# Second mixers of a state-space block: the first group's convolution as matmuls, side work re-laid, the matrix of means as one column

## What is computed

```
xi, z = split(x @ Win)                  # 512 channels each
xi = silu(causal_dwconv(xi, convw) + convb)          # 4 taps a channel
dt, B, C = split(xi @ Wx); dt = softplus(dt @ Wdt + bdt)
h[t] = exp(dt[t] * A) * h[t-1] + dt[t] * xi[t] * B[t]     # 16 states a channel
y[t] = sum over states of C[t] * h[t] + D * xi[t]
out = (y * silu(z)) @ Wout
```

## Time and profile before

| | |
|---|---|
| median of 3 runs | 3392.23 us (3391.65 to 3394.02) |
| profiled execution | 3390.75 us, its span 3389.0 us |
| DVE busy | 2789.4 us, 82% |
| PE busy | 2772.9 us, 82% |
| POOL busy | 2236.3 us, 66% |
| ACT busy | 1774.9 us, 52% |
| TensorE's granted clock, mean | 0.93 |

### The profile page before, as it was taken

The page is one execution under the profiler, slowest core; times in us unless marked ns, Lnnn a source line. Parts: engine busy times, 40 slices in busy tenths (PEclk is TensorE's granted clock), DMA queues, the critical chain, the costliest instruction groups (busy, mean ns, idle before and its releaser), DMA issues. The chain is left out here.

```text
span 3389.0 us, 25111 instructions
## 1 busy us (share of the span) xinstructions
PE 2772.9 (82%) x7782; PEld 1186.5 (35%) x7782; DVE 2789.4 (82%) x2257; ACT 1774.9 (52%) x2375; POOL 2236.3 (66%) x1102
## 2 busy tenths in 40 slices
PE   7678777765778888988888898898898887688999
PEld 2223222454223333333333333333333332244444
DVE  6999999543369999999999999999999999588200
ACT  6775767222355555655655565565556554234211
POOL 3796499001249898898898899898898999301000
PEclk8999799877889999999999999899999999899999
DMA  2011011156625554554554555554545556321000
GB/s 66 31 50 37 21 54 51 37 193 226 217 90 180 172 182 169 182 186 165 190 193 156 196 184 168 174 186 161 201 174 180 193 175 203 112 68 50 13 19 25
DMA packets 164165, 451.46 MB, mean 133 GB/s; under 512 B 22816, under 2 KB 51680, under 8 KB 164000
## 3 DMA queue, kind: packets, MB, share of 16 engines
q1 hardware_dynamic: 158272, 428.89, 37.2%
q0 software_dynamic: 5760, 20.97, 1.5%
HBM read 414.94 MB, written 34.87 MB: 133 GB/s over the span
## 5 line engine op out<-in xcount | busy, mean ns | idle before, releaser
L1424 POOL TENSOR_TENSOR mix_prod<-mix_spread,mix_h 128x1024 f32<-128x1024 f32 x512 | 1352.9, 2645 | 197.3 <-DVE mix_h L1847 101.6
L1957 PE MATMUL mix_banks<-mix_prod,kept_ident 128*128 128x512 f32 x2048 | 1021.8, 624 | 62.9 <-POOL mix_prod L1424 35.7
L1474 ACT ACTIVATE mix_side_in<-mix_dt,kept_neg_a 128x1024 f32<-128x1024 f32 x384 | 437.5, 1141 | 291.0 <-DVE mix_h L1847 287.1
L1957 PEld LDWEIGHTS mix_banks<-mix_prod,kept_ident 128*128 128x128 f32 x2048 | 396.8, 198 | 482.6 <-issue 303.9
L1833 DVE TENSOR_TENSOR mix_banks<-mix_banks,mix_dtu 128x1024 f32<-128x1024 f32 x384 | 466.9, 1216 | 6.0 <-POOL mix_dtu L1414 3.4
L1847 DVE TENSOR_TENSOR_SCAN mix_h<-mix_side_in,mix_state,mix_banks 128x1024 f32<-128x1024 f32 x192 | 450.6, 2347 | 17.8 <-issue 0.4
L1847 DVE TENSOR_TENSOR_SCAN mix_h<-mix_side_in,mix_banks 128x1024 f32<-128x1024 f32 x192 | 439.0, 2286 | 17.3
L451 POOL TENSOR_TENSOR mix_drive<-mix_drive,mix_du 128x1024 f32<-128x1024 f32 x128 | 304.7, 2396 | 149.9 <-ACT mix_drive L521 149.9
L1434 POOL TENSOR_TENSOR mix_side_in<-mix_spread,mix_dtu 128x512 f32<-128x512 f32 x256 | 326.5, 1275 | 0.1
L1947 PE MATMUL mix_banks<-mix_parts,kept_sel 96*128 96x512 bf16 x384 | 154.0, 401 | 209.0 <-DVE mix_h L1847 201.9
L671 DVE TENSOR_TENSOR_SCAN mix_h<-mix_banks,mix_state,mix_drive 128x1024 f32<-128x1024 f32 x128 | 296.1, 2339 | 11.2 <-POOL mix_drive L451 5.8
(11 more groups left out here) (270 smaller groups left out, 4416.4 us busy)
## 6 DMA issues: line engine op xcount, KB each, us to landing
mix_spread<-par_rows SPq DMA_DIRECT2D x640, 512.0 KB, 4.0
mix_c_row<-c_rows SPq DMA_DIRECT2D x40, 512.0 KB, 3.6
exa_f<-f SPq DMA_DIRECT2D x32, 512.0 KB, 6.8
slot_outputs<-kept_early POOLq DMA_DIRECT2D x32, 512.0 KB, 7.3
ln_zp<-slot_outputs SPq DMA_DIRECT2D x8, 2048.0 KB, 8.4
first_acc<-xT SPq DMA_DIRECT2D x8, 512.0 KB, 7.4
x_scratch<-first_acc POOLq DMA_DIRECT2D x8, 512.0 KB, 3.2
fw_scratch<-mix_res SPq DMA_DIRECT2D x8, 512.0 KB, 5.4
```

The costliest lines, as they stand in the source:

```text
L1424: pool.tensor_tensor(prod[:, un % 2, :], spread[:, i % SLOTS, :], h[:, un % HR, :], ALU.mult).then_inc(prod_ready, 1)
L1474: act.activation(drive[un % 2] if pooled(un) else side_in[:, un % 2, :], dt[:, at // NS, :], ACT.Exp, scale=neg_a[:, way(p), at:at + 1]).t ...
L1957: mm = pe.matmul(y_bank[:, hf, :], k.ident[:], half(prod[:, un % 2, :], hf), start=False, stop=True, skip_group_check=True)
```

## The change

- Group 0's convolution is done like group 3's: four diagonal matrices on PE in slots 29 and 30 of the pass before, two evictions by ACT at slots 30 and 31. tap_diag holds two sets of matrices. The taps of group 0 on ACT and DVE are gone; DVE keeps those of groups 1 and 2 (slots 36, 37, 38 and 39, 41, 42).
- The two z products of group 1 go from slots 29, 30 to 31, 32, and silu_z from 31 to 33. gate_y of group 1 stays at 34.
- The input products go from slots 26, 28, 32, 33, 34, 36, 37, 39 to 24, 27, 33, 34, 35, 36, 38, 39, their evictions with them; the second var from 27 to 28, its roots from 28 to 29.
- On DVE root_of of the second half goes from slot 40 to 35, its two normed from 43, 44 to 40, 43, and one joined from 38 to 44.
- The matrix of means becomes a column of one element a partition, read as 128 columns with step zero.

```diff
             if p + 1 < passes:
-                for n, s in enumerate((26, 28, 32, 33, 34, 36, 37, 39)):
+                for n, s in enumerate((24, 27, 33, 34, 35, 36, 38, 39)):
                     order.append((s, 0, ("xi", p + 1, n // 2, n % 2)))
-                order += [(41, 0, ("cv", p + 1, 0)), (42, 0, ("cv", p + 1, 1))]
+                for g, s in ((0, 29), (3, 41)):
+                    order += [(s + h, 0, ("cv", p + 1, g, h)) for h in range(2)]
...
-        tap_diag = m.sb("tap_diag", [P, KC, P])
+        tap_diag = m.sb("tap_diag", [P, 2, KC, P])
...
             def tap_matrices(way):
-                for t in range(KC):
-                    act.activation(tap_diag[:, t, :], k.ident[:], ACT.Copy, scale=taps[:, way, 3, t:t + 1]).then_inc(taps_ready, 1)
+                for n, g in enumerate((0, 3)):
+                    for t in range(KC):
+                        act.activation(tap_diag[:, n, t, :], k.ident[:], ACT.Copy,
+                                       scale=taps[:, way, g, t:t + 1]).then_inc(taps_ready, 1)
...
-                    if s in (43, 44):
-                        keep_cv(p + 1, s - 43)
-                    for g, s0 in enumerate((29, 34, 37)):
+                    for g, s0 in ((0, 30), (3, 43)):
+                        if s in (s0, s0 + 1):
+                            keep_cv(p + 1, g, s - s0)
+                    for g, s0 in ((1, 35), (2, 37)):
                         if s == s0:
                             first_tap(p + 1, g)
...
-                    for g, at in enumerate(((31, 32, 33), (35, 36, 37), (39, 41, 42))):
+                    for g, at in ((1, (36, 37, 38)), (2, (39, 41, 42))):
                         if s in at:
                             conv(p + 1, g, 1 + at.index(s))
...
-            def conv(p, hf):
-                kept = ("xi", p, 3, 1)
-                bank = into("cv", p, hf)
+            def conv(p, g, hf):
+                kept = ("xi", p, g, 1)
+                bank = into("cv", p, g, hf)
                 pe.wait_ge(free[steps.bank(*kept)], steps.full(*kept))
                 if p in (0, WAY):
-                    pe.wait_ge(taps_ready, KC * (way(p) + 1))
+                    pe.wait_ge(taps_ready, 2 * KC * (way(p) + 1))
                 for t in range(KC):
                     x0 = (PAD - t if way(p) else t) + hf * TT
-                    mm = pe.matmul(bank, tap_diag[:, t, :], x[:, 1, x0:x0 + TT], start=t == 0, stop=t == KC - 1)
-                done(mm, "cv", p, hf)
+                    mm = pe.matmul(bank, tap_diag[:, g // 3, t, :], x[:, g % 2, x0:x0 + TT], start=t == 0, stop=t == KC - 1)
+                done(mm, "cv", p, g, hf)
...
-        k.mean = m.sb("mean", [P, P])
+        k.mean_col = m.sb("mean", [P, 1])
+        k.mean = k.mean_col[:].broadcast_to((P, P))
```

More of the change, by code:

```diff
@@ L1174, in __init__ @@
                     order += [(s, h, ("dt", p, g, h)) for h in range(2)]
-                for g, at in enumerate(((12, 13), (29, 30), (43, 44), (55, 56))):
+                for g, at in enumerate(((12, 13), (31, 32), (43, 44), (55, 56))):
                     order += [(at[h], 2, ("z", p, g, h)) for h in range(2)]
@@ L1521, in keep_cv @@
                     act.wait_ge(full[steps.bank(*last)], steps.full(*last))
-                act.activation(half(u[:, p % 2, 3, :], hf), side_bank(*key), ACT.Identity,
-                               bias=small[:, way(p), 0, 3:4]).then_inc(free[steps.bank(*key)], 1)
+                act.activation(half(u[:, p % 2, g, :], hf), side_bank(*key), ACT.Identity,
+                               bias=small[:, way(p), 0, g:g + 1]).then_inc(free[steps.bank(*key)], 1)
             def tap_matrices(way):
-                for t in range(KC):
-                    act.activation(tap_diag[:, t, :], k.ident[:], ACT.Copy, scale=taps[:, way, 3, t:t + 1]).then_inc(taps_ready, 1)
+                for n, g in enumerate((0, 3)):
+                    for t in range(KC):
+                        act.activation(tap_diag[:, n, t, :], k.ident[:], ACT.Copy,
+                                       scale=taps[:, way, g, t:t + 1]).then_inc(taps_ready, 1)
             def silu_u(p, g):
-                if g < 3:
-                    act.wait_ge(tap_done, p * 9 + 3 * (g + 1))
+                if g in (1, 2):
+                    act.wait_ge(tap_done, p * 6 + 3 * g)
                 else:
                     for hf in range(2):
-                        key = ("cv", p, hf)
+                        key = ("cv", p, g, hf)
                         act.wait_ge(free[steps.bank(*key)], steps.full(*key))
@@ L1637, in side @@
                         roots(p - 1, 0)
-                    if s == 28:
+                    if s == 29:
                         roots(p - 1, 1)
@@ L1642, in side @@
                         tap_matrices(1)
-                    for n, s0 in enumerate((27, 29, 33, 34, 35, 37, 38, 40)):
+                    for n, s0 in enumerate((25, 28, 34, 35, 36, 37, 39, 40)):
                         if s == s0:
                             keep_xi(p + 1, n // 2, n % 2)
-                    if s in (43, 44):
-                        keep_cv(p + 1, s - 43)
-                    for g, s0 in enumerate((29, 34, 37)):
+                    for g, s0 in ((0, 30), (3, 43)):
+                        if s in (s0, s0 + 1):
+                            keep_cv(p + 1, g, s - s0)
+                    for g, s0 in ((1, 35), (2, 37)):
                         if s == s0:
                             first_tap(p + 1, g)
-                for s0, gate, shaped in ((14, 0, ()), (31, 1, ()), (40, None, (0, 1)), (45, 2, (2, 3)), (57, 3, ())):
+                for s0, gate, shaped in ((14, 0, ()), (33, 1, ()), (40, None, (0, 1)), (45, 2, (2, 3)), (57, 3, ())):
                     if s == s0 and (own and gate is not None or ahead and shaped):
@@ L1787, in side @@
                         gate_y(p - 1, 3)
-                    for hf, at in enumerate(((18, 22, 23, 24, 38, 45), (30, 40, 43, 44, 51, 52))):
+                    for hf, at in enumerate(((18, 22, 23, 24, 44, 45), (30, 35, 40, 43, 51, 52))):
                         if s == at[0]:
@@ L1975, in side @@
                         var(p - 1, 0)
-                    if s == 27:
+                    if s == 28:
                         var(p - 1, 1)
                 if ahead:
-                    for n, s0 in enumerate((26, 28, 32, 33, 34, 36, 37, 39)):
+                    for n, s0 in enumerate((24, 27, 33, 34, 35, 36, 38, 39)):
                         if s == s0:
                             xi(p + 1, n // 2, n % 2)
-                    if s in (41, 42):
-                        conv(p + 1, s - 41)
+                    for g, s0 in ((0, 29), (3, 41)):
+                        if s in (s0, s0 + 1):
+                            conv(p + 1, g, s - s0)
                     for n, s0 in enumerate((47, 49, 50, 51)):
```

18 lines of the change are left out of this document (9 added, 9 removed).

## The result

| | before | after |
|---|---|---|
| median | 3391.94 us (3391.53 to 3394.02, 4 runs) | 3431.82 us (3423.03 to 3436.32, 4 runs) |
| profiled execution, its span | 3390.75, 3389.0 us | 3434.66, 3432.9 us |
| DVE busy | 2789.4 us | 2779.3 us |

The change costs 1.15% (ratio 1.0115, 95% interval 1.010 to 1.013). Forecast were 3412 us and at most 3423: the direction was right, the loss (39.9 us) is twice the forecast.

A forecast was written before the change was run, and what follows sets the result against it. DVE was taken to bound the second mixers' passes. PE's chain 9.2, first tap 2.9, lead-in 7.4 and last pass 0.1 summed to 19.6 us, giving 3412 us, 0.6% slower than 3392.23; range 3401 to 3423 us.

The forecast's parts named there:

- the chain of PE: Slots 29 to 34: PE's added blocks delay unit 32's spread and gate_y, net loss 9.2 us over seven passes.
- lead-in: Before the first scan: group 0's convolution on PE delays group 3's, 7.4 us later, bounds 5.2 and 8.6.
- column: Step-zero load of the means: taken as zero cost, ends +7 and -6 us; dear load grouped with a 0.13 rival.
- The first tap of group 1: Slots 35 and 36: DVE waits 0.4 us a pass for ACT's first tap, 2.9 us in seven passes.
- Moved steps keep their cost on DVE: Newton step moved from slot 40 to 35 and normalising steps moved earlier: cost on DVE unchanged, counted as nothing.
- the last pass: Last pass of the second mixers: the moved z may cost 0.1 us.
- the blocks fit: Rival: PE's chain shorter by 5 us or more, neither wait arises, 3375 us, faster; chance 0.08.
- only the spread is late: Rival: unit 31's add does not hold gate_y, a pass keeps 0.5 us, 3396 us; chance 0.11.
- The clock: Rival: PE's clock falls inside the chain, 1.2 us longer a pass, 8.6 us in seven, 3421 us; chance 0.13.

The follow-up runs named there:

- run 3: Changed kernel with one matmul instead of four in each of group 0's two convolution blocks (output differs): 3393.82 us, ratio 1.0004 to the kernel before.
- run 1: Kernel before with only the matrix of means turned into one column read with step zero: 3391.58 us, ratio 0.9997.
- run 2: Kernel before with the side work at the changed kernel's slots, group 0's convolution still on ACT and DVE, full matrix of means: 3418.39 us, ratio 1.0068.
- run 5: Kernel before with one DVE normalising step moved from slot 43 to 41, right ahead of a tap of group 2: 3404.54 us, ratio 1.0040.
- run 6: Changed kernel with taps at slots 37, 38, 39 and 41, 42, 43, normalising steps at 40 and 44, one joining step at 36: 3415.70 us, ratio 1.0065.
- run 4: Changed kernel with DVE's taps one slot later, group 1 at 37, 38, 39 and group 2 at 40, 41, 42: 3428.51 us, ratio 1.0103.

## Why the prediction missed

**Right: the chain of PE.** To copy the same sequence of instructions from slots 41 to 45 of the kernel before gave both stretches within 0.01 us of what came. From the end of scan 26, as the prediction's times imply, the spread of unit 32 was to be complete after 19.15 us and gate_y to begin after 28.65; measured 19.14 and 28.63. DVE's idle time fell at the places named, with PE as releaser (2.1 to 2.6 and 1.9 to 2.0 us a pass), and slots 31 to 34 cost 9.3 us instead of 9.2. That this sum fits so well is partly luck: the first pass costs 2.1 us instead of 1.2, because PE's spread is not the 0.9 us earlier that was counted on (issued 18.52 us after the end of scan 26, 18.54 in the other passes), and the third and fifth cost 1.1 instead of 1.55, because DVE lost 0.4 to 0.5 us just before, in slot 27. Run 3 shows that the waits come from the length of the blocks.

**Right: lead-in and column.** 7.7 us for 7.4, and the first scan at 991.84 of which 2.8 us were late before the stage began; 190 ns and no difference in time (run 1).

**Wrong: the step "The first tap of group 1".** Its wait was sized fairly (0.23 to 0.28 us in six passes for a predicted 0.4; 0.88 in the first). But the step took the tap's own duration, 1.26 us, as fixed. The pause is long enough for POOL to begin its product first, and the tap then lasts 2.0 us longer: 14 us in seven passes. That is the mis-sized term: 2.9 us were predicted, slots 35 to 44 measured 17.6, of them 14.0 by these taps and 2.4 by the waits for ACT; and it was to be at most 0.65 us a pass, where it is 2.3 to 3.6. Shown by run 2 (it comes with the layout alone), by run 5 (a like loss from one moved step in the kernel before) and by run 6 (without it 16 us are back). The rows for it were in the trace of before: the taps in the earlier trace rows never lost the way, but POOL's products beside a tap took 3.3 us instead of 2.35. I had read these rows only as a cost to POOL, the engine with room. And DVE's other side steps with two inputs in SBUF did lose the way there: twelve of them are 0.25 to 1.74 us too long in the second mixers, 9.0 us in all. One of the kernel before, seventh pass, with POOL beside it; such a step lasts 0.73 us elsewhere:

```profile
2527.08 2.47 DVE L1761 SCALAR_TENSOR_TENSOR mix_res<-mix_res,mix_norm_s,mix_logv 128x512 f32<-128x512 f32 x1
```

```profile
2526.64 5.13 POOL L1424 TENSOR_TENSOR mix_prod<-mix_spread,mix_h 128x1024 f32<-128x1024 f32 x2 [2.40 <-PE mix_banks L1957]
```

**Wrong: "Moved steps keep their cost on DVE"**, for the same reason. In this change it did no harm beyond that tap; in run 4 it was most of the 12 us by which my expectation failed.

**Wrong in size: the last pass**, 2.9 us for 0.1. No convolution follows there, yet z of group 1 is behind the spread of unit 32 all the same, and gate_y waits; slots 33 and 34 take 2.6 us more, and slot 30 0.9, where the Newton step waits for ACT. PE, then DVE, last pass:

```profile
2843.32 0.39 PE L1951 MATMUL mix_banks<-mix_parts,kept_sel 96*128 96x512 bf16 x1 [2.54 <-DVE mix_h L1851]
2843.54 0.38 PE L1951 MATMUL mix_banks<-mix_parts,mix_sel_late 96*128 96x512 bf16 x1
2843.76 3.37 PE L1961 MATMUL mix_banks<-mix_prod,kept_ident 128*128 128x512 f32 x4
2846.92 2.13 PE L1897 MATMUL mix_banks<-kept_xn,kept_early 128*128 128x512 f32 x4
```

```profile
2855.11 1.23 DVE L1747 TENSOR_TENSOR mix_u<-mix_banks,mix_u 128x1024 f32<-128x1024 f32 x1 [1.92 <-PE mix_banks L1961]
```

Where z had stood PE now has nothing to do and idles 2.54 us; the add behind that takes 3.37 us instead of 1.88, rows at twice the distance, that is at the lower of the two levels, 1.2 GHz (granted clock 0.50 over 2844 to 2847 us). In run 2 gate_y waits 1.92 us there too. In run 3 PE idles 2.52 us at the same place, but the clock stays (1.00 over 2795 to 2815 us), and gate_y waits 0.80 us: so 0.8 us of the wait come from the order alone, and 1.1 from the clock. What made it fall in one and not in the other I don't know.

**Open: 3.9 us in other slots, and 2.8 ahead of the mixers.** At slots 6, 7 and 24 to 27 single passes gain or lose 0.3 to 1.7 us in every kernel here, also in run 1, where no instruction has moved and the eighth pass is 2.9 us longer than before. Most of it is the same loss again: at slots 7, 24, 25 and 27 side steps with two inputs in SBUF meet POOL in one pass and not in another. The row of 2.47 us above is slot 24 of the seventh pass, and the kernels without it are 1.7 us shorter there. At slots 5 and 6 DVE waits up to 1.1 us for PE's spread instead, again in single passes. In run 5, whose edit is at slot 41, the other slots make the third pass 3.5 us longer. What decides in which pass they meet stays open. The 2.8 us are variation: the mixers' first matmul starts at 927.8 to 934.4 us in the ten traces, in no order of the edits.

**The rivals.** That the blocks fit is excluded by the waits of 2.1 to 2.6 us; that only the spread is late, by the 1.98 us in front of gate_y. The clock did not fall inside the chain: in the third pass the granted clock over 1578 to 1618 us was 1.00, and in all seven passes the spread of unit 32 is issued 18.52 to 18.55 us after the end of scan 26. The column is out by run 1.

## To carry over

A side step of an engine that is the bound has more than a duration and a wait: it has a moment at which it begins beside its neighbour. Where the trace shows a neighbour's instruction stretched beside it, ask what happens if the order of the two turns round; here 0.2 us of pause, or one small step in front, turned 1.26 us into 3.3. And a block of matmuls is hidden by the bound engine's work between two of its inputs from PE: spread such blocks out over slots, remember that work which is removed was also cover, and copy the same sequence's time from elsewhere in the trace, since it held to 0.01 us.
